# A two-layer attention and feed-forward kernel on one core: another order of work in the first attention, and some VectorE scratch tiles laid two elements apart

## The reference

```python
x = x + _L0_xattn_ref(_layernorm(x), ctx_1024, ...)   # first attention, 16 heads of 16
x = x + _L0_ffn_ref(_layernorm(x), ...)               # feed-forward, 256 -> 768 -> 256, fp8-rounded weights
x = x + _L1_xattn_ref(_layernorm(x), ctx_1024, ...)   # second attention, 16 heads of 128
x = x + _L1_ffn_ref(_layernorm(x), ...)               # feed-forward, 256 -> 1024 -> 256
```

```python
q = _ln((x @ Wq + bq).reshape(b, s1, H, HD), qn_w, qn_b)            # a norm over each head's 16 numbers
k = _ln(kv[..., :HD], kn_w, kn_b); v = kv[..., HD:]                 # from the first 48 context rows
k_dca = _ln(kv_dca[:, :, 0], kn_dca_w, kn_dca_b)                    # from the last 16, with other weights
ctx = _attn(q, k, v) + _attn(q, k_dca, v_dca)                       # two softmaxes over 48 and 16 keys
return ctx @ Wo + bo
```

## Time and profile before

| | |
|---|---|
| median of three runs | 774.4 us |
| time of the profiled execution | 776.6 us |
| its span, first to last instruction | 774.7 us |
| TensorE busy | 677.9 us (87%) |
| VectorE busy | 567.3 us (73%) |
| ScalarE busy | 486.5 us (63%) |
| GpSimd busy | 439.0 us (57%) |
| granted TensorE clock, mean | 0.959 |

### The profile page before, as it was taken

The page is one execution under the profiler, slowest core; times in us unless marked ns, Lnnn a source line. Parts: engine busy times, 40 slices in busy tenths (PEclk is TensorE's granted clock), DMA queues, the critical chain, the costliest instruction groups (busy, mean ns, idle before and its releaser), DMA issues.

```text
span 774.7 us, 16352 instructions
## 1 busy us (share of the span) xinstructions
PE 677.9 (87%) x5782; PEld 542.8 (70%) x5782; DVE 567.3 (73%) x1282; ACT 486.5 (63%) x996; POOL 439.0 (57%) x648
## 2 busy tenths in 40 slices
PE   1778788888799989999999999999999999876774
PEld 1556666665688877888888888888888888764331
DVE  3589998896558787767667677676776766728996
ACT  1356666664365667666666666666666666647894
POOL 2477777675567754555656656665666654453200
PEclk9799999895699999999999999999999999999997
DMA  9200000220310100000000000000000000000001
GB/s 277 52 9 8 6 7 9 96 77 1 122 49 9 35 14 1 1 24 20 22 24 12 22 22 22 22 15 16 28 15 22 1 2 2 1 1 2 28 28 55
DMA packets 26019, 22.83 MB, mean 29 GB/s; under 512 B 5041, under 2 KB 24402, under 8 KB 25810
## 3 DMA queue, kind: packets, MB, share of 16 engines
q1 hardware_dynamic: 24688, 21.44, 8.9%
q10 hardware_dynamic: 1250, 0.33, 0.2%
HBM read 19.67 MB, written 2.10 MB: 28 GB/s over the span
## 4 chain that ended last, share of the span: by engine, by line
PE 69%; DVE 13%; ACT 7%; issue 6%; POOL 4%; DMA 1%; SPq 0%; DVEq 0%; ACTq 0%; POOLq 0%
PE banks L1538 12%; PE banks L1251 7%; PE banks L1252 5%; PE banks L1253 5%; PE banks L1617 4%; PE banks L1591 4%; PE banks L1583 4%; PE banks L1547 4%; PE banks L1415 3%; PE banks L1416 3%; PE banks L1394 3%; ACT kT0s L1082 3%; PE banks L1376 2%; PE banks L1287 2%; DVE h_sum L994 2%
## 5 line engine op out<-in xcount | busy, mean ns | idle before, releaser
L674 POOL TENSOR_TENSOR rstd<-var,minus_half 128x8 f32<-128x8 f32 x65 | 107.7, 1657 | 5.1
L650 POOL TENSOR_TENSOR pr<-pr,rstd 128x256 f32<-128x256 f32 x64 | 39.4, 615 | 80.1 <-DVE pr L944 80.1
L665 POOL TENSOR_TENSOR p_n<-pr,pinv 128x256 f32<-128x256 f32 x64 | 39.4, 615 | 79.4 <-DVE pinv L905 79.4
L1538 PE MATMUL banks<-m_hi,z_hi 128*128 128x256 f32 x256 | 75.6, 295 | 7.5 <-DVE z_lo L897 7.4
L1176 ACT ACTIVATE kT<-banks,gk_q 128x512 f32<-128x512 f32 x64 | 44.0, 688 | 53.1 <-PE banks L1547 53.1
L1538 PE MATMUL banks<-m_lo,z_hi 128*128 128x256 f32 x256 | 72.9, 285 | 0.0
L1538 PE MATMUL banks<-m_hi,z_lo 128*128 128x256 f32 x256 | 72.9, 285 | 0.0
L897 DVE TENSOR_TENSOR z_lo<-banks,z_hi 128x512 fp32r<-128x512 f32 x64 | 43.9, 686 | 31.1 <-ACT z_hi L1142 31.1
L940 DVE TENSOR_REDUCE pmax<-banks 128x4 f32<-128x256 f32 x64 | 27.0, 422 | 48.3 <-PE banks L1583 48.3
L924 DVE TENSOR_REDUCE sums<-q_sq 128x4 f32<-128x512 f32 x64 | 43.7, 683 | 25.1 <-ACT q_sq L1157 25.1
L1538 PEld LDWEIGHTS banks<-m_hi,z_hi 128*128 128x128 f32 x256 | 49.1, 192 | 17.5 <-DVE z_lo L897 16.1
(11 more groups left out here) (189 smaller groups left out, 2105.6 us busy)
## 6 DMA issues: line engine op xcount, KB each, us to landing
w_raw<-in_L_xattn_Wq SPq DMA_DIRECT2D x4, 512.0 KB, 5.5
wo_raw<-in_L_xattn_Wo SPq DMA_DIRECT2D x1, 2048.0 KB, 8.3
k_ctx<-in_ctx SPq DMA_DIRECT2D x16, 128.0 KB, 2.7
w_raw<-in_L_ffn_w_gating SPq DMA_DIRECT2D x16, 128.0 KB, 2.4
out_x<-x_sb SPq DMA_DIRECT2D x4, 512.0 KB, 3.0
x_sb<-in_x SPq DMA_DIRECT2D x1, 1536.0 KB, 9.1
a_ctx<-in_ctx SPq DMA_DIRECT2D x16, 64.0 KB, 1.8
w_raw<-in_L_xattn_Wk SPq DMA_DIRECT2D x2, 512.0 KB, 8.2
```

The source lines that it names most:

```text
L650: pool.tensor_tensor(pr[:, 1 - par, :, :], pr[:, 1 - par, :, :], rstd1[:, par, HC:2 * HC].unsqueeze(2).to_broadcast([P, HC, S]), ALU.mult) ...
L674: pool.tensor_tensor(rstd1[:, par, :], var1[:, :], minus_half[:, :].to_broadcast([P, 2 * HC]), ALU.pow).then_inc(root1, 1)
L1538: last = nc.tensor.matmul(bank[6][:, za * D:(za + 1) * D], z[:, odd, c, :], mm[:, h, :], start=w % NS == 0 and c == 0 and m == 0, stop=w % ...
```

## The change

Three things are changed, all in the first attention.

First, three scratch tiles of VectorE and GpSimd get a twin with a last dimension of 2 of which only element 0 is used, so that neighbouring numbers stand 8 bytes apart: `rnd2` for the rounding constants of the first block's weights, `half2` for the halved variances and `rstd2` for the roots. The formulas and instruction counts stay.

Second, stages stand in another order. TensorE turns the rows of tile `i + 3` where it turned those of `i + 2`, and does so later; it makes q and k earlier, and multiplies by `Wo` after it has turned `qk_norm`. VectorE adds tile `i - 2` to `x_sb` behind the subtraction of the maxima where it added tile `i - 1` at the end, and makes the rounding constants last. ScalarE copies `probT` later, takes the exponentials ahead of `oT`, and squares between the long and the short pair of `kT0s`. GpSimd does the weight piece of the tile before, and the bias, ahead of the probabilities. The loop runs from -3 to `NT` + 1, two turns more.

Third, PSUM places move: the values go to the first half of bank 7, their product to the second, and the result of `Wo` to bank 2 (bank 5 for the last tile).

```diff
-        A_FIRST, A_LAST = -2, NT + 1
+        A_FIRST, A_LAST = -3, NT + 2
+        def y_bank(t):
+            return bank[2 if t < NT - 1 else 5]
...
# sbuf
+        rnd2 = sb(sa, "rnd2", [P, 2, W_CHUNK, 2])
+        half2 = sb(sa, "half2", [P, 2, 2 * H, 2])
+        rstd2 = sb(sa, "rstd2", [P, 2, 2 * H, 2])
...
# VectorE
-                    first_guess(dve, LN_N * t + 1, qk_half[:, t % 2, :], qk_mean[:, :], qk_rstd[:, t % 2, :], qk_tmp[:, t % 2, :])
+                    first_guess(dve, LN_N * t + 1, half2[:, t % 2, :, 0], qk_mean[:, :], rstd2[:, t % 2, :, 0], qk_tmp[:, t % 2, :])
...
-                    e4m3_magic(dve, magic_steps, 2 * c, w0_raw[:, c * W_CHUNK:(c + 1) * W_CHUNK], rnd[:, c % 2, :])
+                t = i - 2
+                if live(t, NT):
+                    dve.wait_ge(y_done, t + 1)
+                    dve.wait_ge(x_biased, t + 1)
+                    dve.tensor_tensor(x_sb[:, t, :], y_bank(t)[:, 0:D], x_sb[:, t, :], ALU.add).then_inc(x_updated, 1)
...
+                for c in chunks(i):
+                    after(dve, w0_steps, 2 * (c - 1))
+                    e4m3_magic(dve, magic_steps, 2 * c, w0_raw[:, c * W_CHUNK:(c + 1) * W_CHUNK], rnd2[:, c % 2, :, 0])
...
# GpSimd
-                for c in chunks(i):
+                for c in chunks(i - 1):
                     pool.wait_ge(magic_steps, 2 * c + 2)
...
# ScalarE
+                    turned_keys(t, 0)
                 t = i + 2
                 if live(t, NT):
                     act.wait_ge(cent_ready, t + 1)
                     act.activation(qk_sq[:, :, :], qk_cent[:, t % 2, :, :], ACT.Square).then_inc(sq_ready, 1)
+                t = i + 1
+                if live(t, NT):
+                    turned_keys(t, 1)
...
# TensorE, the product with the values
-                    pe.wait_ge(v_ready, 2 * (t + 1))
-                    after(pe, x_updated, t)
+                    pe.wait_ge(v_ready, 2 * min(t + 2, NT))
```

More of the change, by code:

```diff
@@ L1030, in hi_of, with turned_keys @@
                 act.activation(xT_hi[:, :, cols].rearrange("p k (a n) -> p a k n", a=2), source[:, :].rearrange("p (a k n) -> p a k n", a=2, k=KD), ACT.Copy).then_inc(done, 1)
-            def step(i, k):
-                t = i - 1
-                if live(t, NT):
-                    act.wait_ge(pt_done, t + 1)
-                    after(act, o_done, t)
-                    for half in range(2):
-                        act.activation(probT[:, 4 * half:4 * half + 4, :].rearrange("p c n -> p (c n)"), bank[3 + half][:, :], ACT.Copy).then_inc(pt_evac, 1)
+            def turned_keys(t, seg):
+                keys = bank[3][:, D:2 * D].rearrange("p (e s) -> p e s", s=S)
+                lo, hi = ((0, MAIN), (MAIN, S))[seg]
+                for odd in range(2):
+                    r = key_row(seg, odd)
+                    act.activation(kT0s[:, :, odd, lo:hi], keys[:, :, lo:hi], ACT.Identity,
+                                   scale=cols[:, 0, r:r + 1], bias=cols[:, 0, r + 1:r + 2]).then_inc(t_evac, 1)
+            def step(i, k):
                 t = i + 2
@@ L1058, in step @@
                         act.activation(v_blk[keys, t % 2, :, :, odd * HD0:(odd + 1) * HD0],
-                                       bank[2][keys, 0:D].rearrange("p (b r d) -> p b r d", b=PER, d=HD0), ACT.Copy).then_inc(v_ready, 1)
+                                       bank[7][keys, 0:D].rearrange("p (b r d) -> p b r d", b=PER, d=HD0), ACT.Copy).then_inc(v_ready, 1)
+                if live(i + 3, NT) and i + 3:
+                    normalised(i + 3)
+                t = i - 1
+                if live(t, NT):
+                    act.wait_ge(pt_done, t + 1)
+                    after(act, o_done, t)
+                    for half in range(2):
+                        act.activation(probT[:, 4 * half:4 * half + 4, :].rearrange("p c n -> p (c n)"), bank[3 + half][:, :], ACT.Copy).then_inc(pt_evac, 1)
                 if i == NT:
@@ L1062, in step @@
                         hi_of(n, bank[n], fT_done, fT_hi)
+                t = i
                 if live(t, NT):
@@ L1326, in step @@
                     last.then_inc(qk_done, 1)
[L1327 to L1338 removed]
+                if i == NT:
+                    for n in range(2):
+                        turned(n, bank[n], f_xhat, f_xhat_ready, fT_done, None)
                 if i == 0:
@@ L1354, in step @@
                     last.then_inc(t_done, 1)
+                t = i - 1
+                if live(t, NT):
+                    pe.wait_ge(o_evac, t + 1)
+                    after(pe, x_updated, t)
+                    for kk in range(KD):
+                        last = nc.tensor.matmul(y_bank(t)[:, 0:D], oT[:, kk, :], wo0[:, kk, :], start=kk == 0, stop=kk == KD - 1)
+                    last.then_inc(y_done, 1)
+                t = i + 1
+                if live(t, NT):
                     after(pe, v_ready, 2 * t)
```

130 lines of the change are left out of this document (55 added, 75 removed).

## The result

The changed kernel took 764.9 us (median of five runs, 761.5 to 766.3) against 774.4 before (five runs, 773.1 to 776.6): ratio 0.988, 95% interval 0.986 to 0.990, 9.5 us faster. A second set of six runs, made later as an experiment, gave 764.9 again (ratio 0.987, 0.984 to 0.990). The forecast was 759.0 with 750 to 772: the direction and the range held, and the number was 6 us too low. The mechanism behind it did not hold, as the rows show.

What follows compares the result with a forecast made beforehand. The prediction took VectorE's list, 9.89 us a turn in the first attention, as the bound. Turns 14.2 plus way out 1.6 minus start 0.3 gave 15.5 us: 776.6 profiled to 761.1, or 759 against the median; range 750 to 772.

Steps and rivals of the forecast that it cites:

- VectorE's list: VectorE's instructions in one turn of the first attention: 9.89 us before, setting the turn, and about 8.6 after the change.
- the ring through TensorE: Chain from guess through GpSimd, TensorE and ScalarE to the next scores: 7.9 us, 1.8 slack before; 8.6 after the change.
- Laid two apart: Step of two elements in VectorE's scratch tiles: its guess and rounding instructions no longer wait for GpSimd; list 8.52 us.
- the terms 0.88 and 0.49 us of the sum: VectorE's savings per turn from the step: 0.88 us on the guess (L398, L400), 0.49 on the rounding pair.
- rival B: The step leaves VectorE's collisions with GpSimd, only moved: 9.8 us per turn, 770 to 775 us; chance 0.20.
- The turns: Thirteen turns of the first attention loop, from 10.05 to 8.96 us each: 14.2 us saved.
- The way out: From the last maximum to the first feed-forward matmul: 15.7 instead of 17.3 us, 1.6 saved.
- The start: First two turns of the loop: the square delays the first scores by 0.6 us, partly covered; 0.3 lost.
- the excess of 0.16 us per turn: Mean turn 10.05 against 9.89 us, from GpSimd's roots or a lower TensorE clock; kept in the forecast turn of 8.96.
- TensorE's order: q and k ahead of the product with the values cover the wait for `probT`; TensorE's work 7.95 us per turn.

Runs made afterwards that it cites:

- e3_psum: The changed kernel with the rounding constant and the guess's first values passed through PSUM bank 1, TensorE's next q and k waiting for that: 753.9 us, ratio 0.974.
- e6_old_psum: The kernel before, in its old order, with the rounding constant passed through PSUM bank 4 and the guess's first values through bank 1: 774.0 us, ratio 1.001.
- e1_dense: The changed kernel with its three twin tiles packed again, order and everything else as changed: 763.7 us, ratio 0.987.
- e2_step_old_order: The kernel before with only the three tiles laid two elements apart, in the old order: 772.9 us, ratio 0.999.
- e7_bias_late: The changed kernel with GpSimd's addition of the bias put back behind the probabilities: 769.4 us, ratio 0.996.
- e10_qk_late: e3_psum with TensorE's q and k put back behind the product with the values: 763.4 us, ratio 0.985.

## Why the forecast held and its mechanism didn't

**What bounds the kernel.** That VectorE loses 1.70 us a turn waiting for whole instructions of GpSimd was right: in e3_psum and e6_old_psum the same instructions take 0.19 and 0.42 us beside it. That VectorE's list alone sets the turn was half of it. The prediction read "no idle time named" off one turn; grouped over 60 to 110 us, the trace of before has some:

```profile
L776 DVE TENSOR_REDUCE ssum<-prob 128x16 f32<-128x768 f32 x6 | 5.7, 942 | 0.6 <-ACT prob L1065 0.6
...
L747 DVE TENSOR_REDUCE qk_mean<-qk_sq 128x32 f32<-128x512 f32 x5 | 3.4, 686 | 0.5 <-ACT qk_sq L1088 0.4
```

These are the two places at which e6_old_psum waits 5.0 and 3.1 us. And the ring through TensorE was computed as 7.9 us from guess to scores, with 1.8 us of slack; there is a tighter one, that of `probT` and q and k, with 0.2 to 0.4 us.

**The step that failed** is *Laid two apart*: "If the step takes these instructions out of the mode that collides". It doesn't: with the step, L429 still takes 1.44 us in the new order and L425 1.13 in the old one, and without it the changed kernel is as fast (763.7 us, e1_dense; e2_step_old_order). So the terms 0.88 and 0.49 us of the sum were not given by the step; the guess gave 0.77 by the order, and the pair cost 0.43 more. I chose this outcome at 0.66 over rival B at 0.20 with nothing in the trace against B, and B held. Nor does the step cost VectorE anything: with one end in PSUM 256 numbers took 0.425 us packed and 0.426 two apart. The Trainium skill (Vector Engine (DVE) Microarchitecture Reference, "5.2 Measured stream behaviour") says that a stream runs at its full rate only in runs of two or more adjacent words, and has 1.7 to 2.5 ns per number for the wider hops that it measured. At a step of two words the runs differ from that condition: the same instruction costs the same packed and two apart.

**Rival B** was right in mechanism and too low in gain (it had 770 to 775 us). It had L421 wait 1.5 us for the long half of the probabilities (L429 takes 1.44) and the guess meet less of GpSimd; but it kept "about 1.7 us of loss as now", a turn of 9.8. The loss now is some 1.15 us at L429 and 0.1 at L427, and none at the guess: the turn is 9.51. With the bias late (e7_bias_late) it is 9.81, B's number. So the term that B mis-sized is the guess, which meets nothing rather than less, because the bias that it met goes ahead of the probabilities.

**The turns** were forecast to give 14.2 us and gave 8.4 and 5.5. **The way out** was forecast at 1.6 and gave 3.5 and 3.2. The exponentials' place alone gives 1.6 (they start 2.65 and 2.85 us behind the last maxima, against 5.24), and I had taken back too much for a TensorE at half clock: in the second execution the granted clock was 0.55 from 181 to 195 us, hardly above the 0.50 of before, and the way out was still 3.2 shorter. **The start** was forecast at a loss of 0.3 and gained 1.1 and 0.7. What is left of the excess of 0.16 us per turn: nothing, twelve turns are 9.51. So a term too large by 6 to 9 us met two terms too small by 3 together, and the total came out 6 us from the forecast. That it lay inside the range is luck: the turns gave what they gave by another mechanism, and the ends of the loop made up a part of what was missing.

**TensorE's order** did what the prediction said (the wait for `probT` covered), but little of its worth can show while L429 waits: without it the ring takes 9.57 us (e10_qk_late), hardly more than the turn of 9.51 that the changed kernel has anyway. The changed kernel with this move alone undone was not run. Where the collisions are gone, the move is worth 0.94 us a turn (e10_qk_late against e3_psum). The order and the detours need each other: the detours in the old order gain nothing (e6_old_psum), the new order without them some 10 us, both but this one move 11 (e10_qk_late), both in full 20 (e3_psum).

**Open:** which of the moves at the start and end of the loop gives what is left there (1.7 us of the way out, 0.7 to 1.1 at the start), and why TensorE's granted clock was lower in the last turn of one execution (11.0 us) and not of the other (8.1). The longer matmuls of that turn account for the difference; what lowered the clock was not tried.

## What to carry to other kernels

In these traces a one-source VectorE instruction (`tensor_scalar`) from SBUF to SBUF stands still until the GpSimd instruction that runs beside it has ended, packed or two elements apart (1.44 us where 0.29 are its own); the way out is to place it where GpSimd is idle, or to give it one end in PSUM, at 0.42 us instead of 0.29 for 256 numbers but without the wait. A change of layout in the same change as a new order should be priced by a run with the layout alone. Before the waits in the list of a full engine are counted as gain, the next bound is to be found: look for idle time at any instruction of that engine over several turns, and for the rings that close without it.

## What the runs showed that I had not expected

- Two elements apart, 256 numbers from SBUF to SBUF took 0.26 and 0.29 us, and 0.234 on average in e7_bias_late (L427), more than one number per ns in each partition: the step takes nothing from VectorE's speed, and nothing from its wait. What it costs is on GpSimd, 0.04 us a turn.
- Taking an instruction away can be worth no more than making it shorter: with nearly all pairs left out the turn was 8.90, with the pair in PSUM 8.91, with the guess in PSUM as well 8.63. What counts is which GpSimd instruction the next one meets.
- With work taken from VectorE in the old order (e6_old_psum) TensorE's granted clock was lower over 60 to 110 us (0.90 against 1.00 before), and there were turns of up to 12.2 us, so that the mean turn was 10.02 (54.53 to 184.84 in 13), as before (10.05). That the one brought about the other is not shown.
